# Rounding the fp4 weights inside the combine phase: all of the first two parts ahead of the rounds, lower halves as subtractions on GpSimd, the factor 64 moved into the step and the scaling

## The chip, the cores and the metric

One core of one Trainium2 chip runs the whole program. The metric is the device time of one execution in microseconds, taken as the median of several executions. The traces below come from one profiled execution of the kernel before, whose own time stands in the table.

## What is computed

Two layers on 8192 tokens of width 256. Layer 0 is linear attention, gated by a mixture of 16 experts with a Lorentz residual; layer 1 is retention, gated by a feed-forward net whose weights and inputs are rounded to fp4 in blocks of 16. What the change touches is the rounding of the three weight matrices of that net (`w_gate`, `w_up`, `w_down`), which do not depend on the tokens:

```python
scale = jnp.max(jnp.abs(xb), axis=-1, keepdims=True) / 6.0
scale = jnp.maximum(scale, jnp.float32(1e-12))
xn = xb / scale
idx = jnp.searchsorted(_MID, jnp.abs(xn))
q = _GRID[idx] * jnp.sign(xn) * scale
...
h = jax.nn.silu(gate) * y
return fp4_linear(h, w_down)
```

Matrix products are made of fp16 pairs: an upper half (the value times 64, rounded to fp16) and a lower half (the value times 64 minus the upper half).

## The kernel before

The program is a chain of phases with barriers between them: a front, a dense phase, the experts, **the combine phase** (`phase_combine`, tile names `both_...`), then the layer 1 phases (`ffn`, `ret`, `out`). Only the combine phase is touched. Nothing in it is planned by a scheduler: every engine walks the same 20 rounds, written out without loops, and semaphores tie the engines together.

There are 16 groups of 512 tokens. Round i works on several groups at once, each one step further on:

- GpSimd (POOL) gathers the rows of the first expert of group i into `y` (four indirect DMAs), then those of the second expert into `ob` (four more). There are two `ob` buffers, so the second half of group t waits for `s_y1`, which VectorE (DVE) raises when it has merged group t-2 (`second`).
- ScalarE (ACT) weighs `ob` of group i-1, takes sums of squares of groups i-2 and i-3 (`squares`), and the gate of group i-4.
- DVE does, in this order, `second(i-2)`, `third(i-3)`, half of `result(i-4)`, `first(i-1)`, `inner`, `roots` (a chain of 11 tiny instructions, each waiting for the one before it), the other half of `result` and `add_input(i-4)`. After those come the pieces of the weight rounding.
- TensorE (PE) makes the output projection and, from round 9 on, transposes the rounded weights (`pe_turn`), which ACT copies out (`act_evacuate`).
- SyncE (SP) issues the plain loads and stores.

`WeightRounding` cuts the weights into 6 parts (`STEPS`) of 128 x 704 (four of gate and up, two of down). One part n passes through: a load into one of two windows `win` (SP); `dve_scale` (largest of each block, step, reciprocal, scaled values into `val`); `act_magic` (ACT); `dve_round` (round, grid, value); `act_hi` (the upper half, ACT); and `dve_low` (the lower half). `val` has two buffers, so the scaling of part n waits for the lower half of part n-2:

```python
dve.wait_ge(self.lo, free(t))
dve.scalar_tensor_tensor(self.b3(self.work[u]), self.b3(src), 1 - 2.0 ** -22, ...)
```

Which round does which piece stands in four tables at the top of `phase_combine`: `scaled_at` (scaling), `rounded_at` (magic and rounding), `low_at` (upper and lower half) and `turned_at` (transposes).

Of the kernel before, what the change touches and what calls it, by code (L numbers as in the profile page):

```python
# [46 lines left out]
FF = 704  # L47
# [57 lines left out]
def done(t):  # L105
    return t.n + (LAG + 1)
# [7 lines left out]
def free(t):  # L114
    return t.n + 1
# [332 lines left out]


class WeightRounding:  # L450

# [7 lines left out]
    def __init__(self, ph, ps, w_dram, ident, GU, DN):  # L459
# [4 lines left out]
        self.dn_lo = ph.sb("dn_lo", [P, self.DN_TILES, FFC * P], F16)  # L464
        self.fq = Quant(ph, "fq", FF, WS)
        self.s_win = [ph.sem(f"win{n}") for n in range(self.STEPS)]
# [28 lines left out]
    def dve_begin(self, dve):  # L495
        self.fq.prime_dve(dve)
        self.fq.prime_low(dve)
        dve.memset(self.dn_lo[:], 0.0).then_inc(self.fq.filled, 1)
        dve.wait_ge(self.fq.filled, 2)
# [14 lines left out]

    def dve_low(self, dve, n):
        self.fq.low(dve, self.tile(n), self.part16(n, 0), self.part16(n, 1))

# [3 lines left out]
    def act_hi(self, act, n):  # L521
        t = self.tile(n)
        if n >= self.GU_STEPS:
            act.wait_ge(self.fq.xq, done(t))
            again = self.dn_hi[:, n - self.GU_STEPS, FF:2 * FF]
            act.activation(again, self.fq.shaped(t, again), ACT.Copy, scale=WS)
        self.fq.act_hi(act, t, self.part16(n, 0))
# [1286 lines left out]
def phase_combine(nc, ps, oT_all, wq, B_out, ones2, ident, x_dram, w_fp4, GU, DN, z_dram, rows_dram,  # L1814
# [9 lines left out]
    with Phase(nc, "both") as ph:  # L1824
# [17 lines left out]
        weights = WeightRounding(ph, ps, w_fp4, ident, GU, DN)  # L1842
        scaled_at = {0: 0, 1: 1, 3: 2, 6: 3, 9: 4, 12: 5}
        rounded_at = {i + 1: n for i, n in scaled_at.items()}
        low_at = {i + 2: n for i, n in scaled_at.items()}
        turned_at = {9 + n // 2: tuple(m for m in (n, n + 1) if m < weights.gu_groups)
# [26 lines left out]
        def _(sp):  # L1873
# [10 lines left out]
            def store(t):  # L1884
                sp.wait_ge(s_x1, t.n + 1)
                sp.dma_start(views[2][t.n], y[:, t.n % ROWS]).then_inc(s_store[t.n % ROWS], 16)
            for n in range(weights.WIN):
                weights.sp_load(sp, n)
# [33 lines left out]
        @block.gpsimd  # L1922
        def _(pool):

            def gather(t, pos, dst, slot, arrived, tiles=range(G)):
                for k in tiles:
                    at = bass.IndirectOffsetOnAxis(ap=pos[:, t.n * G + k:t.n * G + k + 1], axis=0)
                    pool.indirect_dma_start(dst[:, slot, k], None, rows_dram, at).then_inc(arrived[slot], 16)  # L1928

            def gather_first(t):  # L1930
                if t.n >= ROWS:
                    pool.wait_ge(s_store[t.n % ROWS], 16 * (t.n // ROWS))
                gather(t, pos_lo, y, t.n % ROWS, s_ga)

            def gather_second(t, tiles):
                if t.n >= SECOND:
                    pool.wait_ge(s_y1, t.n - SECOND + 1)
                gather(t, pos_hi, ob, t.n % SECOND, s_gb, tiles)

            for i in rounds:  # L1940
                if group(i):
                    gather_first(group(i))
                if group(i):
                    gather_second(group(i), range(0, 2))
                if group(i):
                    gather_second(group(i), range(2, G))

        @block.scalar
        def _(act):
            weights.fq.prime_act(act)  # L1950

            def second_weighted(t):
# [47 lines left out]
        def _(dve):  # L2000
# [91 lines left out]

            weights.dve_begin(dve)
            for i in rounds:
                if group(i - 2):
# [11 lines left out]
                if group(i - 4):  # L2107
                    result(group(i - 4), 1)
                    add_input(group(i - 4))
                if i in low_at:  # L2110
                    weights.dve_low(dve, low_at[i])
                if i in rounded_at:
# [633 lines left out]
```

## Time and profile before

| | |
|---|---|
| median of 3 executions | 1734.18 us (1731.83 to 1741.62) |
| the profiled execution's own time | 1735.38 us |
| its span in the trace | 1733.6 us |
| share of the span that each engine is busy | PE 78%, DVE 80%, ACT 70%, POOL 67% |
| the combine phase | 655 to 893 us of the span |
| of these 238 us, busy | DVE 179.1, POOL 130.3, ACT 126.6, PE 93.8 us |

The shares are means over phases with different limits; for this change only the last two lines of the table matter, since every edit lies inside the combine phase and barriers close it on both sides. POOL's descriptor work for a gather is counted as busy, the pause of 0.3 us between two of them is not.

### The profile page before, as it was taken

What the parts mean: (1) busy time and instruction counts of PE and PEld (TensorE: products, weight loads), DVE (VectorE), ACT (ScalarE), POOL (GpSimd) and SP (SyncE); (2) the same over time, 40 slices, a digit from 0 to 9 for tenths busy, and PEclk for the clock granted to TensorE, in tenths of its full rate; (3) what the DMA queues carried; (4) which work ended last, traced back from release to release, by engine and by line L of the source; (5) the groups of instructions that cost most, each with busy time, mean ns of one, the idle gap of its engine ahead of it and who ended that gap; (6) DMA issues with size and microseconds to landing.
All of it is one profiled execution on the core that took longest, in us unless ns stands there. A gap on an engine that the chain in (4) does not pass through costs nothing. (4 is left out here: it accounts for less than half of the span.)

```text
span 1733.6 us, 63736 instructions
## 1 busy us (share of the span) xinstructions
PE 1354.2 (78%) x21833; PEld 952.0 (55%) x21834; DVE 1383.5 (80%) x3719; ACT 1216.7 (70%) x3356; POOL 1165.7 (67%) x1293
## 2 busy tenths in 40 slices
PE   3539999979999971245426999999987899999847
PEld 2515555557777751123313666666664566666646
DVE  7878888868888765687858999999984788888748
ACT  7817888858778763456747888888754677777645
POOL 6838888734443446565416999999974687787747
PEclk9999999989999996566758999999999999999969
DMA  8727778779998895476534666666653222222238
GB/s 257 238 86 178 205 207 204 202 158 193 202 215 205 196 195 189 147 230 211 184 103 97 128 126 134 128 131 124 119 107 56 49 51 54 54 50 53 50 104 292
DMA packets 495357, 256.27 MB, mean 148 GB/s; under 512 B 359358, under 2 KB 484865, under 8 KB 494721
## 3 DMA queue, kind: packets, MB, share of 16 engines
q1 hardware_dynamic: 482658, 219.11, 52.7%
q0 software_dynamic: 12576, 35.67, 6.6%
q8 instruction: 60, 0.98, 0.2%
q14 instruction: 63, 0.51, 0.1%
HBM read 79.52 MB, written 73.44 MB: 88 GB/s over the span
## 5 line engine op out<-in xcount | busy, mean ns | idle before, releaser
L242 PE MATMUL ps<-all_late,l_xq_T 128*128 128x352 f16 x1536 | 252.3, 316 | 54.6 <-DMA l_xq_T<-l_apart 34.3
L242 PEld LDWEIGHTS ps<-all_late,l_xq_T 128*128 (+1 forms) x1536 | 146.7, 99 | 146.7 <-DVE ffn_h L812 39.5
L242 PE MATMUL ps<-l0moe_W,all_xT_all 128*128 128x16 f16 (+2 forms) x1152 | 190.1, 312 | 30.4 <-ACT all_xT_all L1021 22.3
L1594 POOL TENSOR_TENSOR all_late<-experts_se,all_mhalf 128x4 f32<-128x4 f32 (+1 forms) x77 | 76.4, 992 | 173.8 <-DVE experts_se L1784 164.3
L242 PE MATMUL ps<-l_Wq,all_xT_all 128*128 128x256 f16 x384 | 81.3, 375 | 125.0 <-DVE both_y L2042 102.8
L2437 POOL TENSOR_TENSOR all_late<-ret_pm,all_late 128x512 f16<-128x512 f32 x128 | 145.5, 1158 | 19.3 <-ACT all_late L2343 19.3
L242 PEld LDWEIGHTS ps<-l0moe_W,all_xT_all 128*128 128x128 f16 x1152 | 83.7, 100 | 113.2 <-ACT all_xT_all L1021 26.0
L650 PE MATMUL ps<-all_late,ffn_hT 128*128 128x256 f16 x1088 | 130.9, 275 | 9.9 <-ACT l_xq_T L714 6.0
L242 PEld LDWEIGHTS ps<-l_Wq,all_xT_all 128*128 128x128 f16 x384 | 47.6, 130 | 149.7 <-DVE both_y L2042 108.2
L650 PEld LDWEIGHTS ps<-all_late,ffn_hT 128*128 128x128 f16 x1088 | 106.5, 99 | 29.7 <-issue 7.5
L242 PE MATMUL ps<-moe_E,experts_gT 128*128 x864 | 115.6, 274 | 0.0
L2365 DVE TENSOR_TENSOR ret_pm<-ps,l_apart 128x1024 f32<-128x1024 f32 x64 | 78.4, 1225 | 38.0 <-PE ps L2210 23.3
L393 POOL TENSOR_TENSOR ffn_h<-ffn_fq_val,ffn_h 128x704 f16<-128x704 f32 x64 | 97.6, 1525 | 14.3 <-ACT ffn_h L388 14.2
L242 PE MATMUL ps<-l_W,all_xT_all 128*128 128x512 f16 x384 | 95.1, 385 | 2.5 <-DVEq L2133 2.5
L1928 POOL DMA_INDIRECT both_ob<-rows_dram,moe_pos_hi x64 | 63.8, 997 | 48.5 <-DVE both_y L2022 32.7
L2306 ACT ACTIVATE all_xT_all<-ps 128x256 f32 (+1 forms) x64 | 24.6, 384 | 93.4 <-PE ps L2270 93.4
L2325 ACT ACTIVATE all_late<-ps,l_apart 128x512 f16<-128x512 f16 x128 | 81.4, 695 | 12.0 <-PE ps L2225 11.9
L242 PEld LDWEIGHTS ps<-moe_E,experts_gT 128*128 128x128 f16 x864 | 79.4, 98 | 14.8 <-issue 1.3
L1964 ACT ACTIVATE both_junk<-both_y 128x255 f16<-128x255 f32 x128 | 51.4, 403 | 47.3 <-issue 39.0
L242 PE MATMUL ps<-moe_E,experts_hT 128*128 x432 | 70.3, 279 | 17.2 <-issue 8.2
L1928 POOL DMA_INDIRECT both_y<-rows_dram,moe_pos_lo x64 | 66.5, 1039 | 23.4 <-issue 19.2
L2431 POOL TENSOR_TENSOR ret_q<-ret_qd,ret_q 128x256 f16<-128x256 f32 x64 | 43.0, 672 | 58.0 <-ACT ret_q L2338 52.5
(308 smaller groups left out, 4575.6 us busy)
## 6 DMA issues: line engine op xcount, KB each, us to landing
rows_dram<-all_late SPq DMA_DIRECT2D x72, 256.0 KB
ret_v<-ret_vpad SPq DMA_DIRECT2D x256, 64.0 KB
front_xin<-x SPq DMA_DIRECT2D x16, 512.0 KB, 5.1
x_dram<-front_x SPq DMA_DIRECT2D x16, 512.0 KB
all_late<-x_dram SPq DMA_DIRECT2D x64, 128.0 KB
z_dram<-all_late SPq DMA_DIRECT2D x64, 128.0 KB
both_zin<-z_dram SPq DMA_DIRECT2D x16, 512.0 KB
both_xin<-x SPq DMA_DIRECT2D x16, 512.0 KB
```

Source lines behind the costliest of these rows:

```text
L242: mm = pe.matmul(out, lhs[a], rhs[b], start=first and n == 0, stop=last and n == 2, skip_group_check=True)
L393: eng.tensor_tensor(lo, self.shaped(t, hi), hi, ALU.subtract).then_inc(self.lo, 1)
L650: ins = pe.matmul(down_ps, hT[:, t.slot, c % both], DN[:, c], start=c == 0, stop=c == both + FFC - 1, skip_group_check=True)
L1594: pool.tensor_tensor(rows[:, n % 4, which, :, 0], se[:, u, which], power[:, which], ALU.pow).then_inc(s_time, 1)
L1928: pool.indirect_dma_start(dst[:, slot, k], None, rows_dram, at).then_inc(arrived[slot], 16)
L1964: ins = act.activation(junk[k][:, g, 1:D], y[:, t.n % ROWS, g, 1:D], ACT.Square, accum_out=ss[:, i % LAG, k, g:g + 1])
L2306: act.activation(yT_all[:, bass.ds(t.n, 1)].rearrange("p o c m -> p (o c) m"), yps, ACT.Copy, scale=1 / Y_SCALE).then_inc(s_yev, 1)
L2325: ins = act.activation(kx16[:, t.slot4].rearrange("p a c s e j -> p (a c s) e j")[:, :, e], src, ACT.Copy, scale=parity[:, e:e + 1])
L2365: dve.tensor_tensor(pm[:, t.slot4], sps, causal[:].unsqueeze(1).to_broadcast([P, 4, RC]), ALU.mult).then_inc(s_p, 1)
L2431: pool.tensor_tensor(q16[:, u, 1], qd[:, u], q16[:, u, 0], ALU.subtract).then_inc(s_qlo, 1)
L2437: ins = pool.tensor_tensor(p16[:, u, 1, r], pm[:, u, r], p16[:, u, 0, r], ALU.subtract)
```

## The change

The first two parts are scaled, and rounded, before round 0, one after the other on DVE; four windows' loads are issued ahead of the rounds on SP. The other four parts follow in rounds 2, 4, 7 and 10 instead of 3, 6, 9 and 12. The lower half goes from DVE to POOL, two rounds behind the upper half, ahead of that round's gathers. The factor 64 now sits in the step and in the scaling, so that `val` already holds 64 times the value: the upper half is a plain copy and the lower half a plain subtraction.

```diff
+class QuantScaled(Quant):
+    def dve_step(self, dve, t):
+        u = t.slot
+        dve.wait_ge(self.am, done(t))
+        dve.tensor_scalar(self.step[:, u], self.amax[:, u], WS / 6, WS * 1e-12, ALU.mult, ALU.max).then_inc(self.st, 1)
+
+    def dve_scale(self, dve, t, src):
+        u = t.slot
+        dve.wait_ge(self.rs, done(t))
+        dve.wait_ge(self.lo, free(t))
+        dve.scalar_tensor_tensor(self.b3(self.work[u]), self.b3(src), WS * (1 - 2.0 ** -22),
+                                 self.wide(self.rstep[u]), ALU.mult, ALU.mult).then_inc(self.v, 1)
...
-        self.fq = Quant(ph, "fq", FF, WS)
+        self.fq = QuantScaled(ph, "fq", FF, 1.0)
...
-        self.fq.prime_low(dve)
...
-    def dve_low(self, dve, n):
-        self.fq.low(dve, self.tile(n), self.part16(n, 0), self.part16(n, 1))
+    def pool_low(self, pool, n):
+        if n == 0:
+            pool.wait_ge(self.fq.filled, 2)
+        self.fq.low(pool, self.tile(n), self.part16(n, 0), self.part16(n, 1))
...
-            act.activation(again, self.fq.shaped(t, again), ACT.Copy, scale=WS)
+            act.activation(again, self.fq.shaped(t, again), ACT.Copy)
...
-        scaled_at = {0: 0, 1: 1, 3: 2, 6: 3, 9: 4, 12: 5}
+        FIRST = weights.WIN
+        scaled_at = {2: 2, 4: 3, 7: 4, 10: 5}
         rounded_at = {i + 1: n for i, n in scaled_at.items()}
-        low_at = {i + 2: n for i, n in scaled_at.items()}
+        low_at = {1: 0, 2: 1}
+        low_at.update({i + 2: n for i, n in scaled_at.items()})
...
-            for n in range(weights.WIN):
+            for n in range(2 * FIRST):
                 weights.sp_load(sp, n)
...
+            weights.fq.prime_low(pool)
             for i in rounds:
+                if i - 2 in low_at:
+                    weights.pool_low(pool, low_at[i - 2])
                 if group(i):
                     gather_first(group(i))
...
             weights.fq.prime_act(act)
+            for n in range(FIRST):
+                weights.act_magic(act, n)
...
             weights.dve_begin(dve)
+            for n in range(FIRST):
+                weights.dve_scale(dve, n)
+            for n in range(FIRST):
+                weights.dve_round(dve, n)
             for i in rounds:
...
-                if i in low_at:
-                    weights.dve_low(dve, low_at[i])
                 if i in rounded_at:
                     weights.dve_round(dve, rounded_at[i])
                 if i in scaled_at:
```

On DVE, between the last of `roots` of round 2 and the first instruction of round 3 (`both_weight`, in `second(1)`), there stood in the kernel before (`both_fq_val` is `val`, `both_gu16` holds the halves):

```order
L2088 SCALAR_TENSOR_TENSOR both_norm<-both_part,both_norm 128x8
L395 SCALAR_TENSOR_TENSOR both_gu16<-both_fq_val,both_gu16 128x704
L369 SCALAR_TENSOR_TENSOR both_fq_val<-both_fq_big,both_fq_val 128x704
L375 SCALAR_TENSOR_TENSOR both_fq_val<-both_fq_big,both_fq_val 128x704
L383 TENSOR_TENSOR both_fq_val<-both_fq_val,both_fq_step 128x704
L2018 TENSOR_TENSOR both_weight<-both_norm,moe0_w_lo 128x4
L2022 SCALAR_TENSOR_TENSOR both_y<-both_y,both_weight,both_ob 128x256 x4
```

At the same place on DVE in the changed kernel:

```order
L2112 SCALAR_TENSOR_TENSOR both_norm<-both_part,both_norm 128x8
L336 TENSOR_REDUCE both_fq_amax<-both_win 128x44
L456 TENSOR_SCALAR both_fq_step<-both_fq_amax 128x45
L347 RECIPROCAL both_fq_rstep<-both_fq_step 128x44
L462 SCALAR_TENSOR_TENSOR both_fq_val<-both_win,both_fq_rstep 128x704
L2042 TENSOR_TENSOR both_weight<-both_norm,moe0_w_lo 128x4
L2046 SCALAR_TENSOR_TENSOR both_y<-both_y,both_weight,both_ob 128x256 x4
```

The lower half of part 0 and the rounding of part 1 have left this place, and the scaling of part 2 has come from the end of round 3 to the end of round 2. Its last row, L462, is the one that waits for the lower half of part 0.

On POOL, from the start of the phase, the changed kernel issues these rows (L1947 is the gather; the rows `both_y` and `both_ob` of one round stand in a pair, so the first subtraction opens round 3):

```order
L1947 DMA both_y<-rows_dram,moe_pos_lo 128x256 x4
L1947 DMA both_ob<-rows_dram,moe_pos_hi 128x256 x4
L1947 DMA both_y<-rows_dram,moe_pos_lo 128x256 x4
L1947 DMA both_ob<-rows_dram,moe_pos_hi 128x256 x4
L1947 DMA both_y<-rows_dram,moe_pos_lo 128x256 x4
L1947 DMA both_ob<-rows_dram,moe_pos_hi 128x256 x4
L393 TENSOR_TENSOR both_gu<-both_fq_val,both_gu 128x704
L1947 DMA both_y<-rows_dram,moe_pos_lo 128x256 x4
L1947 DMA both_ob<-rows_dram,moe_pos_hi 128x256 x4
L393 TENSOR_TENSOR both_gu<-both_fq_val,both_gu 128x704
```

In the kernel before POOL had only the gathers. Now L393 stands behind the gathers of the rounds before it, and behind what these wait for; four more L393 follow at the head of rounds 6, 8, 11 and 14.

## Rows read from the trace of the kernel before

**Rows 1.** Busy time by stretch: us, each engine's busy us (instructions), PE clock, DMA share, GB/s
```profile
687.00:706.00 19.00, 0.00 (x0) 0.00 (x0) 2.63 (x17) 5.37 (x14) 12.01 (x13) 0.50 0.50 152
722.00:889.00 167.00, 80.76 (x456) 53.71 (x456) 139.70 (x450) 103.14 (x342) 85.91 (x84) 0.68 0.63 198
```

**Rows 2.** Who waited for whom on POOL, 655 to 893 us: us, times, longest
```profile
POOL both_ob L1928 <- DVE both_y L2022: 32.7, 12, 8.7
```

**Rows 3.** Timeline of DVE, rounds 0 to 2: start, us, instruction, [idle before <-releaser]
```profile
658.45 0.89 DVE L336 TENSOR_REDUCE both_fq_amax<-both_win 128x44 f32<-128x704 f32 x1 [1.28 <-DMA both_win<-w_fp]
...
662.67 0.16 DVE L2006 SCALAR_TENSOR_TENSOR both_grow<-both_y,moe_w_lo 128x4 f32<-128x4 f32 x1 [1.67 <-DMA both_y<-rows_dram,moe_pos_lo]
...
665.46 0.88 DVE L369 SCALAR_TENSOR_TENSOR both_fq_val<-both_fq_big,both_fq_val 128x704 f32<-128x704 bf16 x1
...
668.11 0.88 DVE L336 TENSOR_REDUCE both_fq_amax<-both_win 128x44 f32<-128x704 f32 x1
...
670.52 0.15 DVE L2018 TENSOR_TENSOR both_weight<-both_norm,moe_w_lo 128x4 f32<-128x4 f32 x1
...
675.66 0.16 DVE L2006 SCALAR_TENSOR_TENSOR both_grow<-both_y,moe_w_lo 128x4 f32<-128x4 f32 x1 [3.08 <-DMA both_y<-rows_dram,moe_pos_lo]
...
678.90 0.88 DVE L395 SCALAR_TENSOR_TENSOR both_gu<-both_fq_val,both_gu 128x704 f16<-128x704 f32 x1
```

**Rows 4.** Timeline of DVE, rounds 3 to 5
```profile
682.36 0.15 DVE L2018 TENSOR_TENSOR both_weight<-both_norm,moe_w_lo 128x4 f32<-128x4 f32 x1
...
684.69 1.67 DVE L2034 SCALAR_TENSOR_TENSOR both_y<-both_y,both_norm,both_zin 128x256 f32<-128x256 f32 x4
...
687.78 0.17 DVE L2010 TENSOR_TENSOR both_headsq<-both_grow,moe_w_lo 128x4 f32<-128x4 f32 x1 [1.34 <-DVE both_grow L2006]
...
706.06 0.89 DVE L395 SCALAR_TENSOR_TENSOR both_gu<-both_fq_val,both_gu 128x704 f16<-128x704 f32 x1
...
709.27 0.16 DVE L2018 TENSOR_TENSOR both_weight<-both_norm,moe_w_lo 128x4 f32<-128x4 f32 x1
...
713.65 0.16 DVE L2010 TENSOR_TENSOR both_headsq<-both_grow,moe_w_lo 128x4 f32<-128x4 f32 x1
...
717.43 0.68 DVE L2042 SCALAR_TENSOR_TENSOR both_y<-ps,both_y 128x512 f32<-128x512 f32 x1
...
721.95 0.15 DVE L2018 TENSOR_TENSOR both_weight<-both_norm,moe_w_lo 128x4 f32<-128x4 f32 x1
```

**Rows 5.** Timeline of POOL around its longest wait
```profile
687.95 0.94 POOL L1928 DMA_INDIRECT both_y<-rows_dram,moe_pos_lo  x1 [0.30 <-issue]
...
701.72 0.94 POOL L1928 DMA_INDIRECT both_y<-rows_dram,moe_pos_lo  x1 [0.30 <-issue]
711.41 1.18 POOL L1928 DMA_INDIRECT both_ob<-rows_dram,moe_pos_hi  x1 [8.74 <-DVE both_y L2022]
```

**Rows 6.** Timeline of SP: the load that waits for DVE's L2034
```profile
687.07 0.37 SPq L1877 DMA_DIRECT2D both_zin<-z_dram  x1
```

**Rows 7.** Groups of DVE, 655 to 893 us: count, busy us, mean ns, idle before
```profile
L395 DVE SCALAR_TENSOR_TENSOR both_gu<-both_fq_val,both_gu 128x704 f16<-128x704 f32 x4 | 3.5, 884 | 0.0
```

**Rows 8.** Source line L393 in a later phase: the same subtraction on POOL, min/median/max ns
```profile
L393 POOL TENSOR_TENSOR ffn_h<-ffn_fq_val,ffn_h x64: 1515/1524/1538, 949.5 to 1305.9; 128x704 f16<-128x704 f32 x64
```

**Rows 9.** Timelines of DVE and POOL in two later phases
```profile
1402.90 0.89 DVE L2407 SCALAR_TENSOR_TENSOR ret_state<-ret_told,l_apart 128x64 f32<-128x64 f32 x1
...
1402.55 2.29 POOL L2437 TENSOR_TENSOR all_late<-ret_pm,all_late 128x512 f16<-128x512 f32 x2 [0.28 <-ACT all_late L2343]
...
1722.60 1.70 DVE L2535 TENSOR_TENSOR out_x<-out_prod,out_x 128x1024 f32<-128x1024 f32 x1
...
1725.66 1.23 DVE L2535 TENSOR_TENSOR out_x<-out_prod,out_x 128x1024 f32<-128x1024 f32 x1
```

**Rows 10.** Timeline of DVE, start of rounds 15 and 16
```profile
846.93 0.15 DVE L2018 TENSOR_TENSOR both_weight<-both_norm,moe_w_lo 128x4 f32<-128x4 f32 x1
...
856.95 0.15 DVE L2018 TENSOR_TENSOR both_weight<-both_norm,moe_w_lo 128x4 f32<-128x4 f32 x1
```

## The prediction

> **What bounds the kernel now.** All edits lie between two barriers, so I read only the combine phase, 655 to 893 us. Three views, in this order.
>
> First the busy time by stretch. From 722 to 889 us DVE is busy 139.7 of 167 us, ahead of ACT (103.1) and POOL (85.9) [rows 1]. The timeline shows that what DVE doesn't fill there is small change between dependent instructions. A round without weight work is 10.02 us long on DVE [rows 10]; POOL's eight gathers follow each other at 1.25 us (11 of them from 687.95 to 701.72) [rows 5], 10.0 us, which is nearly the same. POOL nevertheless waits 32.7 us for DVE's L2022 in 12 places [rows 2], because DVE's rounds with weight work are longer. So in the steady part DVE sets the pace and POOL is close behind.
>
> Second DVE's timeline of rounds 0 to 2. Before round 2 DVE isn't the bound: it waits for the gathered rows, 1.67 us at 662.67 and 3.08 us at 675.66 [rows 3].
>
> Third the same timeline of round 3, which is where the phase loses most. From L2010 at 687.78 to L395 at 706.06 DVE needs 18.28 us for what it does from 713.65 to 717.43, 3.78 us, one round later [rows 4]. With the 1.34 us of idle time before 687.78 that is 15.8 us too much (1.3 + 14.5). In these 19 us DVE is busy 2.6 us and PE not at all [rows 1]. It isn't DVE's own queue that is slow, but how late others hear of it: L2034 ended at 686.36, and the load on SP that waits for it started at 687.07 [rows 4, 6]. POOL gathers without a pause until 702.66, then waits 8.74 us; the stretch is over 3.4 us after POOL's last gather [rows 4, 5]. No row names the cause. I call it the slow stretch; what becomes of it matters more than any instruction that the change moves.
>
> **The change, part by part.**
>
> *Two parts ahead of the rounds.* A scaling takes 2.41 us (668.11 to 670.52), a rounding 2.65 (665.46 to 668.11) [rows 3]. Two of each from 658.45: 10.1 us, to 668.6. ACT's two magic passes lie under the second scaling and the first rounding. `first(0)` and `roots` take 2.8 (662.67 to 665.46), and `second(0)` 2.0 more: 673.4. The next instruction, at 675.66, waits for a gather that POOL issues as early as before. So 675.66 stays, covered by 2.2 us; without that cover the prologue would cost 3.2 us. DVE reaches the end of `roots` in round 2 at 678.9 as before [rows 3]. The two extra loads on SP stand ahead of the first `zin` load, which isn't needed before round 3: nothing.
>
> *A new wait in round 2.* Then come the block maxima, step and reciprocal of part 2 (1.6 us, to 680.5) and L462, which waits for the lower half of part 0. That one stands on POOL behind all gathers of round 2. These run without a pause from the start of the phase, and the next gather starts at 687.95 in the trace of before [rows 5]; now the subtraction starts there. It takes 1.52 us on POOL [rows 8], against 0.88 on DVE [rows 7]: 689.5. L462 takes 0.8 more, and round 3 begins at 690.3 instead of 682.36 [rows 4]: **+7.9 us**. Queued behind L462 on DVE is everything: `second(1)`, and through it ACT's squares and POOL's gathers of round 3. There is nothing to hide it, because DVE has no other work in its order.
>
> *Rounds 3 and 4.* Round 3 loses a lower half and a scaling (0.8 + 2.4) and gains a rounding (2.65): −0.55. Round 4 loses a rounding and gains a scaling: −0.25. The wait of part 3's scaling (end of round 4) for lower half 1 costs nothing: POOL does that one near 700, DVE asks near 712.
>
> *The four later lower halves* leave DVE at 0.80 us each (678.90 to 679.71, the shift of the next start): −3.2. The scaling of part 3 leaves round 6: −2.4. The rest of the table only trades places.
>
> *What a lower half on POOL costs DVE.* In the output phase L2535, whose two inputs both lie in SBUF, takes 1.70 us while POOL's subtractions run and 1.23 once they are over; in the retention phase L2407, with 64 elements, takes 0.89 us from 1402.90 and ends at 1403.79, about when the first of POOL's two L2437 (2.29 us from 1402.55, 1.15 each) ends [rows 9]. So DVE stands still until POOL's instruction has read its inputs. In the combine phase POOL starts its second four gathers 2.14 us into a round (711.41 against 709.27), and four take 5.2: the subtraction falls at 7.4 to 8.9 us of the DVE round. `roots` ends at 8.16 (717.43) [rows 4, 5]; its tiny instructions all read SBUF twice, and `add_input` behind them too. Bounds: 0 if none meets it; 1.3 us if one is blocked nearly whole (the rows allow 1.5, less the last 0.2 us in which L2407 ran again). DVE issues one such instruction every 0.2 us there, so I take 1.3, five times: +1.3 in round 3 (lower half 1 meets the rounding there) and +5.2 later.
>
> The Trainium skill says the same, and it speaks against this change: "SBUF — State Buffer", section "Who interferes with whom", has it that a DVE instruction with two SBUF inputs and a GpSimd instruction that reads SBUF exclude each other for the whole instruction. By that rule each moved subtraction is a loss of about 0.5 us, not a gain of 0.8; by this trace too.
>
> *The factor 64* changes constants only; no instruction gets longer: 0.
>
> **Sum.** 7.9 − 0.55 + 1.3 − 0.25 = +8.4 at the start of round 5; −3.2 − 2.4 + 5.2 = −0.4 after it: **+8.0 us** if the slow stretch stayed as it is. With free subtractions it is +1.5.
>
> **What the slow stretch does.** If it is tied to POOL's unbroken gathering, as its end suggests, it comes back. DVE then enters it about 694 (`third` of round 3 over). POOL's queue runs from 689.5 through 4 gathers (694.8), 4 more (699.8), a subtraction with its pause (1.8) and 4 more (706.7), and then waits for `second(2)` of round 4. With 3.4 us behind that, the stretch ends at 710.1: 16 us long instead of 19.8, so 3.8 less is lost. +8.0 − 3.8 = +4.2. The profiled execution took 1735.4, which gives 1739.6; it was 1.2 above the median, so **1738**.
>
> **Rivals.**
> - *The stretch is gone.* For it: DVE's rounds have moved by 8 us, no other stretch of the phase loses as much, and POOL now has pauses from gathering. Against it: it came in DVE's round 3 at a place that has the same instructions around it now. +8.0 − 15.8 = −7.8: 1726 on the median's scale. Chance 0.28.
> - *The stretch is gone and the subtractions collide little.* The rows with a collision are instructions longer than those of `roots`; if these slip through, 6.5 us less than the last: 1720. Chance 0.12.
> - *Slower.* POOL, which stopped at 702.66, now has work until 706.7 and later; if the stretch ends by its number of instructions, or follows POOL's queue into round 4, it keeps its 15.8 us or grows, and the new wait of 7.9 us in round 2 stands beside it in full. From 1735.4 + 8.0 − 1.2 = 1742 upwards, 1747 with one more round's 4 to 5 us; it decides for slower as soon as the stretch isn't shorter than before. Chance 0.20.
> - My forecast, shortened stretch: chance 0.40, its own range 1733 to 1744.
>
> That the new wait isn't there is the way in which the whole sum would be wrong: if lower half 0 were done before 680.5. POOL's order excludes it.
>
> **How the numbers follow.** A measurement of this kernel can't tell less than about 0.5% from no change: 1725.5 to 1742.9. Range: from the least of the second rival, 1720, to 1747. Faster: half of the first rival and nearly all of the second, 0.24. Slower: most of the last rival and a little of the forecast, 0.24. The rest, 0.52, is no change.
>
> **What would show it.** In DVE's timeline, L462 of round 2 starts near 689.5 with some 9 us of idle time before it, ended by POOL's L393; the first two scalings and roundings end by 669; the gather's landing at 675.7 still starts `first(1)`. L393 on POOL takes 1.5 us, and a tiny L2110 to L2112 or L2072 under it lasts about 1 us longer. Round 3 shows whether the stretch is there: `roots` with 1.4 us from start to start, or 0.2. The forecast is wrong if the round begins well before 690, if round 5 begins elsewhere than near 726, or if rounds 5, 7, 10 and 13 aren't about 1 us longer than their instructions.

## The result, and the profile after

The changed kernel took 1725.34 us (median of 8 executions, 1720.93 to 1735.17) against 1739.01 for the kernel before (8, 1731.83 to 1743.30) on the same chip: ratio 0.9941, 95% interval 0.992 to 0.9962, **faster by 0.6%**. (The ratio isn't the quotient of the two medians, which is 0.9921.) The profiled execution was the longest of its eight, 1735.17 us, while that of before, 1735.38, lay 3.6 under its median. All lengths of the combine phase below run from DVE's first memset in it to the last instruction on one of its tiles: 232.8 us before, 224.8 after.

The other phases were not edited; dense alone took 5.1 us more in this trace than in that of before (256.7 against 251.6). So whole traces are not compared to a few us; the phase is.

Busy time by stretch: the first row covers 19 us from round 2's last wait into round 4 (answers to the first of [rows 1]), the second the steady part.

```profile
691.00:710.00 19.00, 0.00 (x0) 0.00 (x0) 14.17 (x41) 9.86 (x32) 15.62 (x14) 0.50 0.49 153
727.00:885.00 158.00, 73.93 (x442) 50.59 (x442) 135.90 (x415) 96.98 (x320) 90.76 (x85) 0.68 0.60 195
```

DVE was busy 2.63 us of the 19 that [rows 1] show; now it is 14.17. DVE's timeline, rounds 0 to 5 (answers to [rows 3, 4]; L2030 is `first`, L2042 the start of `second` and so of a round):

```profile
662.98 0.89 DVE L336 TENSOR_REDUCE both_fq_amax<-both_win 128x44 f32<-128x704 f32 x1 [1.44 <-DMA both_win<-w_fp]
...
673.28 0.15 DVE L2030 SCALAR_TENSOR_TENSOR both_grow<-both_y,moe_w_lo 128x4 f32<-128x4 f32 x1
...
679.67 1.67 DVE L2046 SCALAR_TENSOR_TENSOR both_y<-both_y,both_weight,both_ob 128x256 f32<-128x256 f32 x4 [3.41 <-ACT both_ob L1981]
...
693.88 0.89 DVE L462 SCALAR_TENSOR_TENSOR both_fq_val<-both_win,both_fq_rstep 128x704 f32<-128x704 f32 x1 [6.57 <-POOL both_gu L393]
694.69 0.15 DVE L2042 TENSOR_TENSOR both_weight<-both_norm,moe_w_lo 128x4 f32<-128x4 f32 x1
...
698.47 0.16 DVE L2034 TENSOR_TENSOR both_headsq<-both_grow,moe_w_lo 128x4 f32<-128x4 f32 x1
...
702.86 0.88 DVE L369 SCALAR_TENSOR_TENSOR both_fq_val<-both_fq_big,both_fq_val 128x704 f32<-128x704 bf16 x1
...
704.70 2.24 DVE L383 TENSOR_TENSOR both_fq_val<-both_fq_val,both_fq_step 128x704 f32<-128x704 f32 x1
706.87 0.15 DVE L2042 TENSOR_TENSOR both_weight<-both_norm,moe_w_lo 128x4 f32<-128x4 f32 x1
...
719.30 0.15 DVE L2042 TENSOR_TENSOR both_weight<-both_norm,moe_w_lo 128x4 f32<-128x4 f32 x1
```

L462 waits for POOL as predicted (it starts 33.4 us after the phase's start, 33.5 were predicted), and round 3 starts 34.2 us after the phase's start instead of 26.4: +7.8. But from 698.47 to 702.86 DVE needs 4.4 us for what took 18.28 in [rows 4]. The slow stretch isn't there. POOL's first and third subtraction (answer to [rows 5]), and DVE under the third:

```profile
692.26 1.52 POOL L393 TENSOR_TENSOR both_gu<-both_fq_val,both_gu 128x704 f16<-128x704 f32 x1
...
728.01 1.53 POOL L393 TENSOR_TENSOR both_gu<-both_fq_val,both_gu 128x704 f16<-128x704 f32 x1
```
```profile
727.17 0.17 DVE L2111 SCALAR_TENSOR_TENSOR both_part<-both_sq,both_diff 128x12 f32<-128x12 f32 x1
727.38 2.20 DVE L2112 SCALAR_TENSOR_TENSOR both_norm<-both_part,both_norm 128x12 f32<-128x12 f32 x1
```

A tiny instruction of 0.17 us takes 2.20: it begins 0.63 us before POOL's recorded start and ends with POOL's end. POOL's waits for `second` (answers to [rows 2], 32.7 us in 12 places there):

```profile
POOL both_ob L1947 <- DVE both_y L2046: 10.0, 5, 2.4
```

### The profile page after: what moved, and what is told of

It is laid out like the page before. It is cut to its first block and busy times, and to the rows that moved or that the text cites. A ratio compares the mean times of both kernels' runs of the same rounds, so it can differ in the third digit from the quotient of the medians.

```text
span 1733.4 us, 63737 instructions
## 1 busy us (share of the span) xinstructions
PE 1356.7 (78%) x21833; PEld 952.4 (55%) x21834; DVE 1388.8 (80%) x3713; ACT 1215.3 (70%) x3356; POOL 1181.3 (68%) x1299
## 5 line engine op out<-in xcount | busy, mean ns | idle before, releaser
L242 PE MATMUL ps<-l_Wq,all_xT_all 128*128 128x256 f16 x384 | 76.1, 357 | 124.3 <-DVE both_y L2066 92.9
L393 POOL TENSOR_TENSOR ffn_h<-ffn_fq_val,ffn_h 128x704 f16<-128x704 f32 x64 | 97.5, 1523 | 15.0 <-ACT ffn_h L388 14.9
L2351 ACT ACTIVATE all_late<-ps,l_apart 128x512 f16<-128x512 f16 x128 | 81.3, 694 | 12.8 <-PE ps L2251 12.7
L1947 POOL DMA_INDIRECT both_y<-rows_dram,moe_pos_lo x64 | 69.4, 1084 | 22.6 <-issue 18.3
L1947 POOL DMA_INDIRECT both_ob<-rows_dram,moe_pos_hi x64 | 64.6, 1010 | 28.0 <-issue 18.0
```

What stands on the lines that cost most here:

```text
L242: mm = pe.matmul(out, lhs[a], rhs[b], start=first and n == 0, stop=last and n == 2, skip_group_check=True)
L393: eng.tensor_tensor(lo, self.shaped(t, hi), hi, ALU.subtract).then_inc(self.lo, 1)
L2351: ins = act.activation(kx16[:, t.slot4].rearrange("p a c s e j -> p (a c s) e j")[:, :, e], src, ACT.Copy, scale=parity[:, e:e + 1])
```

## The experiments

The runs fall into five sets (e1 to e4, e5 to e8, e9 to e12, e13 to e16, e17 and e18). Each set ran on one chip with the kernel before beside it, the first two sets on the same chip, so on four chips in all. On two of them the kernel before took 1741 to 1745 us, on two 1711 to 1712. Which chip the result above comes from isn't known; with 1739.01 it is like the first two. "Phase" is the length of the combine phase in the one trace of the run. "Ratio" is to the kernel before of the same set. A traced execution can lie far from its median (e12 6.4 us above, e7 1.6 above, e17 3.2 and e18 4.9 below), so phases of different runs compare to some us only.

| run | before, us | this, us | ratio (95%) | phase |
|---|---|---|---|---|
| e1 before again | 1745.2 | 1745.2 | | 242.9 |
| e2 low on DVE | 1745.2 | 1740.1 | 0.9978 (0.9963 to 0.9993) | 238.3 |
| e3 old order | 1745.2 | 1743.5 | 0.9992 (0.9974 to 1.0009) | 241.4 |
| e4 low 0 earlier | 1745.2 | 1734.1 | 0.9951 (0.9934 to 0.9968) | 229.0 |
| e5 POOL pause | 1743.9 | 1730.6 | 0.9917 (0.9896 to 0.9939) | 227.9 |
| e6 before, paced | 1743.9 | 1733.1 | 0.9942 (0.9924 to 0.996) | 229.5 |
| e7 low on DVE, paced | 1743.9 | 1734.3 | 0.9931 (0.9912 to 0.995) | 228.5 |
| e8 after again | 1743.9 | 1727.6 | (one execution) | 227.8 |
| e9 low on DVE, pause each | 1741.3 | 1728.3 | 0.9921 (0.9908 to 0.9934) | 225.4 |
| e10 before, pause each | 1741.3 | 1727.5 | 0.9923 (0.9905 to 0.9941) | 226.7 |
| e11 before, 0.1 us each | 1741.3 | 1742.0 | 1.0004 (0.9992 to 1.0015) | 241.0 |
| e12 no subtraction | 1741.3 | 1733.6 | 0.9956 (0.9939 to 0.9972) | 234.0 |
| e13 after, pause each | 1712.4 | 1731.3 | 1.0111 (1.0092 to 1.013) | 230.8 |
| e14 low 0 earlier, pause each | 1712.4 | 1729.0 | 1.0096 (1.0077 to 1.0115) | 230.6 |
| e15 before, 0.5 us each | 1712.4 | 1712.1 | 1.0004 (0.9992 to 1.0017) | 214.1 |
| e16 before, one pause | 1712.4 | 1713.0 | 1.0003 (0.9991 to 1.0015) | 212.5 |
| e17 after, timed | 1711.2 | 1720.3 | 1.0057 (1.0042 to 1.0071) | 220.9 |
| e18 low on DVE, timed | 1711.2 | 1709.9 | 0.999 (0.998 to 1.0) | 208.8 |

### First set: the parts of the change

**e1_before_again**: the kernel before, unedited.

> The unchanged kernel before, for one more trace. If the slow stretch of round 3 belongs to this order of work, DVE again needs about 18 us from L2010 to L395 of round 3 (the trace before: 18.28) against 3.8 us a round later, and the combine phase is again near 233 us. If it comes by chance, the stretch is missing or stands elsewhere and the phase is near 217 us.

The stretch is there again, longer: round 3 takes 26.4 us, round 2 15.5, and smaller late spots stand in rounds 6, 9 and 12. By a late spot I mean a place where the chained instructions of `roots` or their neighbours start 0.5 us or more after the end of the one they depend on, where elsewhere 0.04 pass. That the update which tells of the end comes late is my reading of these rows; no row shows its cause.

**e2_low_on_dve**: the changed kernel with the lower halves back on DVE.

```diff
-                if i - 2 in low_at:
-                    weights.pool_low(pool, low_at[i - 2])
...
+                if i in low_at:
+                    weights.pool_low(dve, low_at[i])
```

> The changed kernel with its lower halves back on DVE, right behind the rounds' other work, in the round of the upper half. Theory A (POOL's subtractions cost DVE more than they take from it): the 6.6 us wait of L462 in round 2 goes, four blockings of about 2.0 us and one of 1.35 go, six lower halves of 0.8 us come back: combine phase 225 - 6.6 - 9.4 + 4.8 = about 214 us, ratio to the kernel before about 0.988. Theory B (taking the lower halves off DVE is a gain): the phase gets longer than 225 us, ratio above 0.994.

Wrong by 24 us: no wait before L462 and no held instruction, but round 3 takes 26.1 us. With POOL gathering without a break, the stretch is back; its first late spot comes at 33.7 us of the phase, just after the place where the changed kernel has its first subtraction (31.8).

**e3_old_order**: before's order of parts (`scaled_at = {0: 0, 1: 1, 3: 2, 6: 3, 9: 4, 12: 5}`, nothing ahead of the rounds), subtractions on POOL, factor 64 as changed.

> The order of parts of the kernel before (parts scaled in rounds 0, 1, 3, 6, 9, 12, nothing ahead of the rounds), the lower halves on POOL and the factor 64 as in the changed kernel. If the two parts ahead of the rounds are what removes the slow stretch, it is there again in round 3 (18 us for what takes 4) and the ratio to the kernel before is 1.00 to 1.005. If the moved lower halves remove it, the stretch is missing and the ratio is below 0.997.

Rounds 2 and 3 take 16.2 and 24.2 us, so the stretch is back, and with it the time of the kernel before (0.9992). POOL's first subtraction comes at 42.2 us. Before it one wait of 1.48 us breaks the gathers, from 35.8 to 37.2 us, with the stretch already there since 23 us; late spots go on to 51 us. A pause of this length inside the stretch doesn't end it at once.

**e4_low0_earlier**: lower half 0 ahead of round 2's gathers instead of behind them.

```diff
-                if i - 2 in low_at:
+                if i - 2 in low_at and low_at[i - 2] > 0:
                     weights.pool_low(pool, low_at[i - 2])
+                if i == 2:
+                    weights.pool_low(pool, 0)
```

> The changed kernel with the lower half of part 0 one round earlier on POOL (ahead of round 2's gathers instead of round 3's). The idle time before L462 of round 2 (6.57 us in the trace of the changed kernel) goes. If DVE sets the pace there, round 3 starts 6 to 7 us earlier and the combine phase takes about 218 us instead of 225, ratio about 0.990. If POOL's gathers set it, the time is only shifted: another wait of the same length for gathered rows follows, and the ratio stays at 0.994. A third outcome is that the slow stretch comes back, with 15 us more.

The third outcome: the wait before L462 is gone (round 2 takes 13.0 us, not 18.6), and yet nothing is won over the changed kernel: round 5 takes 20.7 us instead of 14.7, with chained instructions that wait for one another again. POOL had gathered since its subtraction at 44.6 us; the late spot begins at 60.9.

### Second and third set: is it POOL's unbroken gathering?

**e5_pool_pause**: e2, and on POOL, at the place of the subtraction, behind the same wait, a memset that lasts as long.

```diff
+                if i - 2 in low_at:
+                    pool.wait_ge(weights.fq.hi, done(weights.tile(low_at[i - 2])))
...
+                    pool.memset(rest_of[:], 0.0).then_inc(s_rest, 1)
```

> The changed kernel with the lower halves back on DVE (as e2_low_on_dve), and on POOL, where the subtraction stood, a memset of 1792 f16 values (about 1.5 us by the trace's 4096 values in 3.51 us), behind the same wait for ACT's upper half. Theory A (a pause of POOL between gathers is what keeps the slow stretch away): POOL's first burst of gathers ends near 33 us after the phase's start as in the changed kernel, the stretch of 26 us in round 4 is 12 to 13 us, the phase takes 220 to 225 us where e2 took 238, ratio 0.988 to 0.992. Rival B (it is the subtraction's absence from DVE that keeps it away): the phase stays at 236 to 240 us, ratio about 0.998. Lock: if any POOL instruction holds DVE, DVE operations of 2.1 us stand beside the memsets; if only one that reads SBUF does, none.

(What is called e2's round 4 here and below is round 3 in the count used above.) Phase 227.9 against e2's 238.3: rounds 3 to 5 take 11.3, 15.0 and 12.7 us. An instruction that does nothing useful brings 10 us. It doesn't keep every late spot away: round 10 takes 21.6 us, because ACT, idle for 8.26 us, starts a copy of PE's results 7.5 us after PE's last instruction has ended, and DVE waits 6.37 us for what ACT does next.

**e6_before_paced**: the kernel before with a wait that it already has for the upper rows, also for the lower ones.

```diff
                 if t.n >= ROWS:
                     pool.wait_ge(s_store[t.n % ROWS], 16 * (t.n // ROWS))
+                if t.n >= SECOND:
+                    pool.wait_ge(s_y1, t.n - SECOND + 1)
```

> The kernel before with one wait more: POOL gathers the lower rows of group t only after DVE's second() of group t-2, as it already does for the upper rows. POOL then stands still in each round, up to 5 us, from round 3 on. Theory A: no slow stretch, the phase takes 225 to 230 us (before again: 242.9), ratio 0.990 to 0.993. Rival B: the stretch stays, since nothing on DVE or ACT changed: 238 to 243 us, ratio 0.998 to 1.0. Rival D (the gathers arrive too late for first() and for ACT's weighting): waits of DVE for gathered rows of 1 to 3 us in each round, ratio above 1.0.

As theory A had it: no instruction of DVE was touched, and 13.4 us of the phase are gone (229.5 against 242.9; the ratio, 0.9942, is a little above the range). POOL's first wait here, of 3.42 us, ends at 34.3 us of the phase.

**e7_low_on_dve_paced**: e2 with the same wait.

> e2_low_on_dve with the wait of e6_before_paced. Theory A: neither the stretch, nor held operations, nor the wait of L462 for POOL: the phase takes 212 to 220 us (after: 224.8, of which 6.6 the wait and some 8 held operations; plus 3.2 for four lower halves on DVE), ratio 0.984 to 0.990, faster than the changed kernel. Rival B: 235 to 240 us, ratio 0.997 to 0.999. Rival D: as in e6, ratio above 0.998 with waits for gathered rows.

228.5, not 212 to 220. The first wait of POOL begins at 42 us only, and round 3 has 18.4 us, with late spots from 35.9 us on; another stands in round 14 (18.2 us).

**e8_after_again**: the changed kernel once more.

> The changed kernel once more, for a second trace. If the timing of its POOL keeps the stretch away, this one too shows rounds 3 to 5 of 12 to 15 us, a combine phase of 222 to 228 us and a wait of 6 to 7 us before L462 in round 2. If its absence was chance, a stretch of 15 us more stands somewhere in rounds 2 to 6, and the phase takes 235 us or more.

Phase 227.8; round 2 waits 6.57 us before L462 as in the first trace, rounds 3 to 5 take 12.2, 12.4 and 14.7. The absence of the stretch is the kernel's, not one execution's.

**e9_pause_each** (e2) **and e10_before_pause_each** (before): a memset ahead of each group's gathers, with no wait for another engine. **e11_before_tiny_each**: the same with 4 values.

```diff
                 if group(i):
+                    if i:
+                        pool.wait_ge(s_rest, i)
+                    pool.memset(rest_of[:], 0.0).then_inc(s_rest, 1)
                     gather_first(group(i))
```

> e2_low_on_dve (lower halves on DVE) with a memset of 1792 f16 values on POOL ahead of each group's eight gathers, with no wait of its own. It takes no DVE time, moves nothing from DVE and adds no wait. Theory A (a pause between gathers resets what makes updates late): the stretch of e2's round 4 is gone, phase 217 to 225 us against e2's 238.4, ratio 0.986 to 0.990. Rival E (not the pause but a wait of POOL for the other engines, which keeps it from running ahead, is what counts): the stretch stays, 235 us or more, ratio 0.996 to 0.999.

> The kernel before with the same memset on POOL ahead of each group's eight gathers and nothing else: no instruction of DVE, ACT or PE is touched. Theory A: rounds 2 and 3 lose their slow stretch (15.5 and 26.4 us in before again, 12 to 13 each expected), phase 226 to 232 us against 242.9, ratio 0.990 to 0.994. Rival E: phase 240 us or more, ratio 0.998 to 1.001.

> As e10 with a memset of 4 values (0.1 us by its like in the trace) in place of 1792. If any other instruction between gathers suffices, phase and ratio are those of e10. If the pause must be long enough for something to drain, the stretch is there as in before again: 240 us or more, ratio 0.998 to 1.001.

e9 has no late spot in rounds 3 to 5; its phase is 13 us shorter than e2's on the other chip, and its ratio of 0.9921 misses the range expected, 0.986 to 0.990. e10 and e11 came out as theory A had it, and this pair decides. The same 20 us of round 3, on one chip, e11 and then e10:

```profile
688.00:708.00 20.00, 0.00 (x0) 0.00 (x0) 5.22 (x23) 6.96 (x22) 10.96 (x13) 0.50 0.45 133
```
```profile
688.00:708.00 20.00, 3.17 (x14) 1.94 (x14) 17.41 (x57) 13.81 (x47) 16.32 (x16) 0.50 0.59 180
```

DVE busy 5.22 us with a pause of 0.1 us, 17.41 with one of 1.6. What DVE's timeline of e11 shows in it:

```profile
700.36 0.16 DVE L2015 TENSOR_TENSOR both_headsq<-both_grow,moe_w_lo 128x4 f32<-128x4 f32 x1 [7.27 <-remote]
701.76 0.42 DVE L2017 TENSOR_SCALAR both_diff<-both_headsq 128x4 f32<-128x4 f32 x1 [1.24 <-DVE both_headsq L2015]
```

L2015 waits for nothing but the sum that L2011 ended at 693.09, one instruction earlier on the same engine, and starts 7.27 us later; the trace finds no releaser ("remote"). L2017 waits 1.24 us for L2015, which in the changed kernel takes 0.04 (698.47 + 0.16 to 698.67). The memset has a price too. DVE, then POOL, in e10:

```profile
691.51 1.24 DVE L2069 TENSOR_SCALAR both_diff<-both_diff 128x8 f32<-128x8 f32 x1
```
```profile
691.11 1.62 POOL L1946 MEMSET both_rest_of<- 128x1792 f16 x1
```

L2069, a TENSOR_SCALAR of 0.17 us, is held to the end of a memset, which writes SBUF and reads nothing. What the pair doesn't separate is a pause from a lower mean rate of gathers: with 1.6 us more for each eight, POOL also issues them more slowly.

**e12_no_low**: the changed kernel with two memsets (1088 values beside, 704 into the lower half) for each subtraction; the lower halves of the weights are left out.

```diff
-        self.fq.low(pool, self.tile(n), self.part16(n, 0), self.part16(n, 1))
...
+        pool.memset(self.rest_of[:], 0.0).then_inc(self.s_rest, 1)
+        pool.memset(self.part16(n, 1), 0.0).then_inc(self.fq.lo, 1)
```

> The changed kernel with POOL's six subtractions replaced by two memsets each (1088 values beside, 704 into the lower half: about 1.5 us together, writes only); the lower halves of the weights are left out. Same order, same waits, the same pause. The price of the held DVE operations comes out alone: e8 shows three of them at 2.2 us (0.5 and 0.17 usual) on DVE's path. If each costs the path its 1.7 to 2.0 us, the phase is 5 to 8 us below the changed kernel's 224.8 and 227.8, so 218 to 222 us, ratio 0.987 to 0.991. If the holds fall into waits that DVE has anyway, the phase stays within 2 us of it and the ratio is 0.993 to 0.995.

A miss. DVE instructions are held 3.0 us in all instead of 9.4, and the phase is 6 to 9 us longer; the traces come from different chips and from executions 6.4 us (e12) and 9.8 us (the changed kernel) above their medians, but the timed ratio, 0.9956, isn't better than the changed kernel's 0.9941 either. The late spot of e4 stands in round 5 (20.9 us against 14.7), though POOL's pauses lie at 32, 44 and 66 us, nearly as in the changed kernel. One difference in POOL's rows between its second and third pause is this gather of the changed kernel, which takes 1.92 us instead of 0.95 beside two long DVE instructions. e8 and e5 have one of 1.93 us too; in e12 and e4, the two with the late spot, no gather there takes over 1.11:

```profile
715.87 1.92 POOL L1947 DMA_INDIRECT both_ob<-rows_dram,moe_pos_hi  x1 [0.30 <-issue]
```

Whether it matters no run tells. So the price of the holds doesn't come out alone here. What holds what shows in L383, which meets a memset here and met a subtraction above. DVE, then POOL:

```profile
702.27 0.89 DVE L383 TENSOR_TENSOR both_fq_val<-both_fq_val,both_fq_step 128x704 f32<-128x704 f32 x1
...
790.03 2.30 DVE L2114 TENSOR_SCALAR both_norm<-both_seed 128x12 int32<-128x12 int32 x1
```
```profile
702.20 1.03 POOL L538 MEMSET both_rest_of<- 128x1088 f16 x1
...
790.65 1.02 POOL L538 MEMSET both_rest_of<- 128x1088 f16 x1
791.60 0.70 POOL L539 MEMSET both_dn_lo<- 128x704 f16 x1
```

L383 with its two inputs runs through the memset in 0.89 us, under the subtraction it took 2.24. The single-input L2114 is held until the memsets end. In e5, e9, e10 and e12 alike, the held ones are TENSOR_SCALAR instructions, and two-input ones that meet a memset run as always, except where one starts 0.08 us behind a held TENSOR_SCALAR: then both end together (in e10 L2017 from 728.22 and L2061 from 728.30, both to 730.58).

### Fourth and fifth set: chips without the stretch

**e13_after_pause_each** and **e14_early_pause_each** are the changed kernel and e4 with e10's memsets; **e15_before_half_pause** has 512 values in e11's place, **e16_before_one_pause** e10's memset ahead of group 3 alone (`if i == 3:`).

> The changed kernel with e10's memset ahead of each group's gathers, so that neither it nor e10 has the slow stretch: their difference is the change alone. By the prediction's terms without a stretch: +7.9 (L462 waits in round 2 for POOL) - 0.8 - 3.2 - 2.4 + holds of 5 to 9 = +6 to +11 us, phase 233 to 238 against e10's 227.4, ratio 0.996 to 0.999. Rival (holds and wait fall into waits that DVE has anyway, and the work moved pays): phase 224 to 229, ratio 0.990 to 0.993.

> e4_low0_earlier with the same memsets. e4 lost the wait before L462 but a stretch of about 10 us came in round 5, 61 to 71 us after the phase's start, inside a burst of gathers of 73 us. If that stretch was the price of POOL not standing still, it goes: phase 217 to 222 us, ratio 0.986 to 0.990, the best so far. If it was chance or a cost of the order, the phase stays at 226 to 229, ratio 0.992 to 0.995.

> The kernel before with a memset of 512 values (about 0.5 us) ahead of each group's gathers, between e11 (4 values: nothing gained, 1.0004) and e10 (1792: 0.9923). If something must drain, the gain grows with the length: ratio 0.995 to 0.998, the stretch shortened or late. If there is a threshold under 0.5 us: as e10, 0.991 to 0.994. If above it: as e11, 0.999 to 1.001.

> The kernel before with one memset of 1792 values ahead of group 3's gathers alone, about 31 us into the phase. If a pause starts the count of unbroken gathers anew: round 2 as in before again (15.5 us), round 3 of 12 to 14 us instead of 26.4, the small late spots of rounds 6, 9 and 12 unchanged, phase 229 to 233, ratio 0.992 to 0.995. If the pause helps only while it lasts: round 3 stays over 20 us, ratio 0.998 to 1.001.

None of this could be tested as meant: the kernel before itself took 1712.4 us here. The same code over the whole combine phase, e1 and then e16, which has one memset more and, by its ratio of 1.0003, no other time than before:

```profile
653.50:896.50 243.00, 90.52 (x525) 61.08 (x523) 179.12 (x570) 126.67 (x412) 128.92 (x128) 0.65 0.57 180
```
```profile
654.00:866.80 212.80, 95.01 (x526) 63.80 (x523) 182.14 (x570) 126.90 (x412) 137.58 (x129) 0.65 0.65 206
```

DVE has 570 instructions in both and is busy 179 and 182 us; in e16 the phase is 30 us shorter, as is the program (1745.2 against 1712.4). POOL gathers in e16 from 33 to 61 us without a pause, and DVE's waits hold nothing late:

```profile
DVE both_diff L2066 <- ACT both_junk L1968: 11.8, 16, 1.2
DVE both_fq_amax L329 <- PEq L212: 5.1, 1, 5.1
DVE both_grow L2010 <- DMA both_y<-rows_dram,moe_pos_lo: 4.5, 2, 2.9
```

So e15 and e16 say nothing on how long a pause must be or how long it helps. e16's own memset has a price too, which matters when e16 stands in for the kernel before: in round 3 it holds a TENSOR_SCALAR that otherwise takes 0.17 us,

```profile
686.28 1.25 DVE L2068 TENSOR_SCALAR both_diff<-both_diff 128x8 f32<-128x8 f32 x1
```

so from there on the kernel before would be up to 1.1 us ahead of e16.

e13 and e14 give the price of pausing where there is nothing to cure. The wait before L462 grew to 10.5 us in e13 and is gone in e14, yet both phases are 231 us: in e14 DVE waits 9.7 us in 8 places for gathered rows instead (2.4 us in 3 places in e13). By these waits, POOL with its 16 memsets has become the bound.

**e17_after_timed** and **e18_low_dve_timed**: the changed kernel and e2, as they are.

> The changed kernel, timed, on whichever chip comes. Where the kernel before shows the slow stretch (median 1739 to 1745, combine phase 240): as in the result, ratio 0.992 to 0.996. Where it does not (median about 1712, as in the runs beside e13 to e16, phase 212.5 in e16): the change stands without the stretch, and by the prediction's terms costs +8.0 us; phase 219 to 226, ratio 1.004 to 1.008. If there the ratio is 0.998 to 1.001, the terms were wrong and the wait and the holds cost nothing.

> e2_low_on_dve again: the new order of parts and the factor, lower halves on DVE. Where before has the stretch: ratio 0.996 to 0.999 as in e2. Where it has not: no wait before L462 and no holds, so order and factor alone, by the prediction -0.8 us and nothing: ratio 0.999 to 1.001, and the distance to e17 (5 to 9 us) is the price of the lower halves on POOL.

Without the stretch the change is a **loss of 9.1 us** (1.0057); with the lower halves on DVE it is 1.3 us faster (0.999), with an interval of 0.998 to 1.0 that reaches no change. The start of rounds 3, 5 and 17 on DVE in e16, then in e17:

```profile
680.47 0.16 DVE L2022 TENSOR_TENSOR both_weight<-both_norm,moe_w_lo 128x4 f32<-128x4 f32 x1
706.08 0.16 DVE L2022 TENSOR_TENSOR both_weight<-both_norm,moe_w_lo 128x4 f32<-128x4 f32 x1
846.33 0.16 DVE L2022 TENSOR_TENSOR both_weight<-both_norm,moe_w_lo 128x4 f32<-128x4 f32 x1
```
```profile
685.87 0.89 DVE L462 SCALAR_TENSOR_TENSOR both_fq_val<-both_win,both_fq_rstep 128x704 f32<-128x704 f32 x1 [7.16 <-POOL both_gu L393]
686.68 0.15 DVE L2042 TENSOR_TENSOR both_weight<-both_norm,moe_w_lo 128x4 f32<-128x4 f32 x1
711.32 0.15 DVE L2042 TENSOR_TENSOR both_weight<-both_norm,moe_w_lo 128x4 f32<-128x4 f32 x1
853.18 0.15 DVE L2042 TENSOR_TENSOR both_weight<-both_norm,moe_w_lo 128x4 f32<-128x4 f32 x1
```

The phases begin at 654.2 and 652.6. The distances to e16 are +7.8, +6.8 and +8.5 us.

## Why the prediction was wrong

**The failed step is "What the slow stretch does".** The likeliest case, at 0.40, was that the stretch returns, 3.8 us shorter, and leaves +4.2. It didn't return in rounds 3 to 5; the case at 0.28, "the stretch is gone", is what happened. Round 5 begins 58.8 us after the phase's start, where the forecast had 70. That this case's time, 1726, and its −7.8 us are so close to the 1725.34 measured and the −8.0 of the first two traces is partly luck: the timed runs fell by 13.7 us, from a median of 1739.0 that three executions had put at 1734.2, and the second pair of traces on one chip (e8 against e1) gives −15.1. The argument for the return was that POOL's subtractions are too short to matter: I let the queue run through them and added 3.4 us at its end. e10 against e11 shows that a pause of 1.6 us ahead of each group keeps the stretch away and one of 0.1 us doesn't; e5, e6 and e9 show the same with the lower halves elsewhere or with a wait instead. The changed kernel makes such pauses at 32, 44 and 67 us of the phase with its subtractions, and e5 against e2 shows that a memset at these places does the same as the subtraction.

How long POOL must gather before updates come late isn't settled: 15 us after its last pause in e4, 19 in e12, 23 and more after its first gather in before, e1, e2 and e11, while after, e5 and e8 gather 32 us at the start with none. The distance of the pauses alone doesn't order the traces: with pauses at 44 to 45 us and the next 21 to 25 us later, after, e5 and e8 have no late round 3 to 5, and e4 and e12 have one. That is an order of events from single traces, not a threshold.

**The stretch was also sized too small.** I counted 15.8 us, in round 3. On the chips that have it, late updates cost 30 us of the phase in e1 against e16 (242.9 − 212.5), in rounds 2, 3, 6, 9, 12 and the waits between, and 20 us in the very trace that the prediction was read from (232.8 − 212.5). Of these the changed kernel avoids the greater part: 224.8 and 227.8 us there against 220.9 in e17, so 4 to 7 us are left.

**The sum "+8.0 us if the slow stretch stayed as it is" was right for the work itself**, which only e17 could show: +8.4 us of phase against e16, up to +9.5 with the 1.1 us that e16's own memset holds, and +9.1 in the timed runs. Its terms:
- *A new wait in round 2*, +7.9: round 3 starts 7.8 later, in both traces. The idle time was 6.57 and 7.16 us, not 9, because `second(0)` had waited 3.41 us for ACT's weighting and ran late itself (679.67); the end is set by POOL alone.
- *Two parts ahead of the rounds*, hidden: they end at 673.28, 12.8 us after the phase's start, as worked out (668.6 − 656.0 = 12.6). What ends the wait behind them is ACT's weighting, not the gather. Harmless, since POOL sets the end of round 2.
- *Rounds 3 and 4*, −0.55 + 1.3 − 0.25 = +0.5: measured −1.0 (from +7.8 to +6.8) against e16, and about +0.1 without e16's own hold in round 3. The hold of the subtraction is there (L383 at 704.70, 2.24 us for 0.89: 1.35).
- *Later lower halves and part 3's scaling*, −5.6, and four holds: measured +1.7 from round 5 to 17 against −0.4 predicted. The mis-sized term is the hold: 1.9 to 2.0 us of excess in each of four rounds (7.8 us in e17), not 1.3 (5.2), since the instruction is held from before POOL's recorded start. That puts the prediction's −5.6 + 5.2 at −5.6 + 7.8 = +2.2, beside the +1.7 measured.
- *The factor 64*, 0: L462 takes 0.89 us, as the scaling did; no run changed it alone.

The Trainium skill ("SBUF — State Buffer", section "Who interferes with whom") was cited for holds against two-input instructions by a GpSimd instruction that reads SBUF. The runs bear it out in both directions: a two-input L383 is held by the subtraction and not by a memset. The same section has it that a DVE instruction in a two-port mode, which `tensor_scalar` can enter when its operands allow it, contends with GpSimd, and it doesn't limit this to GpSimd instructions that read. e10 and e12 show holds that fit, 0.17 us become 1.24 and 2.30; which mode the held instructions ran in no row shows. That held instructions run to POOL's end is in the rows.

**The slower rival** wanted a stretch that stays. That didn't happen on the first chips; on the chip of e17 there is no stretch, and the sum without it gives the slower side all the same: 1.0057. The profile of one chip could not tell which the next would be. A change of 0.6% could be told from none: the interval of the result is 0.4% wide, where the prediction held less than about 0.5% to be no change.

## What to carry to other kernels

Before costing an edit, look whether the stretch that it moves is made of work or of late updates: here a DVE that was hardly busy, with 0.7 or 1.4 us from start to start of instructions that usually follow each other at 0.2, waited for no data that a row shows, and small shifts on POOL decided what it cost. A change that seems to win there should be tried on more than one chip, and against a dummy (here a memset ahead of each eight gathers in the kernel before, 0.9923) that changes only the timing: this one's gain of 0.6% was such a side effect, and its own work costs 0.6% where the stretch is absent. Moving a subtraction from DVE to POOL doesn't free DVE here: 0.8 us leave it, and a tiny instruction is held 2 us.

## What the runs showed of the hardware

- Two chips of four ran the same program 30 us slower (1745 and 1741 against 1712 and 1711), nearly all of it in the one phase where POOL issues 128 indirect gathers at 1.25 us each while DVE runs short chains. ACT's busy time is the same and DVE's differs by 3 us; DMA moved less per us there (180 against 206 GB/s over the phase). What differs between the chips no run shows, nor whether it is the chip or the occasion: no chip was seen with the stretch and without it.
- On those chips a pause of 1.6 us in POOL's gathers, ahead of each eight, removes the stretch of round 3 and 14 us of the phase (226.7 in e10 against 241.0 in e11); one of 0.1 us removes nothing. Why is open; so are lengths between, since e15 fell on a chip without it.
- On every chip a POOL instruction of 1.5 to 1.6 us holds a DVE instruction from up to 0.7 us before POOL's recorded start to POOL's end: 0.17 us become 2.2. A subtraction holds two-input instructions (5 of 6 times in the changed kernel's first trace; the sixth time DVE was idle) and also a TENSOR_SCALAR (L2088 in e8, 1.99 us), a memset the TENSOR_SCALAR ones and what follows them at 0.08 us (2 of 6 in e12).
- No version that ran is the best on both kinds of chip: without the stretch none is clearly faster than the kernel before (e18, 0.999, is the nearest to it), with the stretch e5, e9 and e10 are the lowest (0.9917 to 0.9923), with intervals that overlap that of the changed kernel. e7's wait with e18's order, 0.9931 with the stretch, wasn't run without it.
